# A perceiver layer with two routed expert stages: one block for both parts, and TensorE in slots of one gated unit with the down product of a unit inside the next

## The chip, the cores and the metric

The kernel runs on one core of one Trainium2 chip. The metric is device time in microseconds (us) of one execution. The core's engines run their own instruction streams in parallel and meet through semaphores: TensorE (PE; PEld is its weight load) for matrix products, VectorE (DVE), ScalarE (ACT), GpSimd (POOL) and SyncE (SP), which here only issues transfers.

## The reference, cut to what matters

`x` is 64 sequences of 32 tokens by 256 channels, so 2048 tokens. One layer is computed: cross attention, a time mix with a first mixture of experts (two choices per token of 8), and a second feed-forward stage with a shared gated unit and one routed gated unit per token:

```python
        def geglu(x, w1, w2, w3):
            return jax.nn.gelu(x @ w1, approximate=False) * (x @ w2) @ w3
        B, T, C = x.shape
        xf = x.reshape(-1, C)
        shared = geglu(xf, w1s, w2s, w3s)
        logits = xf @ Wg
        idx = jnp.argmax(logits, axis=-1)
        final = jnp.zeros_like(xf)
        for e in range(N_EXPERTS):
            y = geglu(xf, W1[e], W2[e], W3[e])
            final = final + jnp.where((idx == e)[:, None], y, 0.0)
        return (shared + final).reshape(B, T, C)
    x = x + _L0_xattn_ref(_layernorm(x, axis=-1), ctx_1024, ...)
    x = x + _L0_attn_ref(_layernorm(x, axis=-1), ...)
    x = x + _L0_ffn_ref(_layernorm(x, axis=-1), ...)
```

w1 and w2 are 256 x 1024, w3 is 1024 x 256, all float32. `_L0_attn_ref` ends in the first mixture of experts. The kernel computes only the chosen expert of each token.

## The kernel before

The 2048 tokens are G = 16 chunks of 128. **Part 1** (cross attention, time mix, first experts in NT1 = 39 tiles of 128 rows) is one block of code; its last steps store expert rows to `rows_y` in DRAM (L476). The block ends with a barrier, the semaphores are cleared (L1486, L1487), and **part 2** follows as three blocks.

The *combine block* (L1722 on) takes a chunk a step. GpSimd copies the chunk's row numbers (L1754) and gathers the two expert rows of each token (`ya`, `yb2`, L1757). VectorE adds them weighted, takes mean and variance; GpSimd takes the inverse root (L1762); VectorE writes the normed `z4` (L1828); SyncE stores it to `rows_z` (L1742). TensorE transposes `z4` into bank `bZ` (L1777), ScalarE copies that to `zT_c` (L1800), and TensorE forms the router's 8 scores (L1785). In the same step TensorE runs the shared unit: `Geglu.hidden` (L1691: 32 products, 64 instructions with the two passes of float32, in two halves of u and g), ScalarE's GELU (L1700), VectorE's product (L1708), and `Geglu.down` (L1715: 8 products). The order on TensorE in a step is hidden products of unit n, transposes of the next chunk, down product of unit n - 1, router. Only SHARED_C = 12 of the 16 chunks have their shared unit here, one step behind; the last four chunks pass through without one.

The *table block* (`routing`) begins when all scores are there. VectorE takes the largest score of each token, counts tokens per expert by two products on TensorE, makes the slot of each token (each expert's rows padded to whole tiles of 128), and builds with one-hot products a table `table2` of which token sits in which row of the NT2 = 23 tiles. One shared unit runs beside it.

The *routed block* takes a tile a step. GpSimd copies a table column (L1920) and gathers 128 rows of `rows_z` (`zr`, L1922). TensorE's order in a step is the 32 hidden products of tile n (weights `we12`), the transposes of tile n + 1 (L1941), the down product of tile n - 1 (weights `we3`); ScalarE copies the transposes (L1979). SyncE loads the expert's weights, 3 MB a tile, two tiles deep (L1893, L1902): the 2 MB of `we12` wait for the hidden products of two tiles before, the 1 MB of `we3` for the down product of two tiles before. Results go to `rows_f` (L1984). One shared unit runs at the front and two at the end. Then GpSimd gathers each token's row of `rows_f` for 16 chunks (L1931), VectorE adds them (L2018), SyncE stores the output (L1913).

In part 1 the lists of tokens are made in another way, which the change takes over: each chunk's token numbers are scattered to a table in DRAM, `tab_e`, by GpSimd (L724); VectorE makes from the counts which expert and which place in the table each tile has (L1348 to L1371); SyncE reads each tile's 128 entries back with an address from a register (`moe_pick`, L344).

`Step` and `sweep` write loops: some steps peeled, the rest in a hardware loop.

## Time and profile before

| | us |
|---|---|
| median of 3 runs | 974.52 (973.53 to 974.78) |
| profiled execution, its own time | 966.43 |
| its span, first to last instruction | 964.7 |
| mean granted clock of TensorE | 0.953 |
| TensorE busy | 858.3 (89%) |
| VectorE busy | 445.0 (46%) |
| ScalarE busy | 316.3 (33%) |
| GpSimd busy | 349.3 (36%) |

Busy time is a union over the instructions of an engine; TensorE's instructions overlap in its pipeline. The granted clock is a share of full speed: 1.00 is the higher of two levels. The profile was taken on an execution of its own, so its span is compared with its own time and not with the median. Part 1 takes the first 485 us, the combine block stands from about 489 to 644, the table block to 668, the routed block to 944, and the last gathers and stores to the end.

### The profile page before, as it was taken

How to read it: one execution, taken by the hardware profiler on the slowest of the kernel's cores; microseconds unless marked ns; L12 is line 12 of the kernel's file. 1: busy time of each engine (PE TensorE's matmuls, PEld its weight loads, DVE VectorE, ACT ScalarE, POOL GpSimd, SP SyncE). 2: the span in 40 equal slices, each digit the busy share in tenths (PEclk: the TensorE clock that was granted, in tenths of full speed). 3: DMA queues.
4: the chain of work that ended last, by engine and by line, in shares of the span. 5: the costliest groups of instructions: out<-in, count | busy, mean ns of one | idle time of the engine just before them, and what ended most of it. 6: DMA issues, size and time to landing. Idle time of an engine off the chain costs nothing. (4 is left out here: it accounts for less than half of the span.)

```text
span 964.7 us, 19179 instructions
## 1 busy us (share of the span) xinstructions
PE 858.3 (89%) x6306; PEld 768.6 (80%) x6306; DVE 445.0 (46%) x1253; ACT 316.3 (33%) x712; POOL 349.3 (36%) x605
## 2 busy tenths in 40 slices
PE   5899989886667999999949999968999999999994
PEld 4567766665566889999849999957999999999993
DVE  1279989888774555555523333353111111111113
ACT  1466767664542445555411111100111111111110
POOL 1445677766775355544142222211100010000006
PEclk9899999998688989999979999989999999999998
DMA  9875557534612322263121111102998988999716
GB/s 355 277 268 189 194 112 233 155 103 188 169 43 53 79 67 83 83 214 84 50 66 33 34 38 40 38 28 73 336 330 305 329 301 324 303 319 306 270 61 175
DMA packets 92096, 161.79 MB, mean 168 GB/s; under 512 B 13832, under 2 KB 71112, under 8 KB 88680
## 3 DMA queue, kind: packets, MB, share of 16 engines
q1 hardware_dynamic: 71008, 103.39, 32.2%
q10 hardware_dynamic: 12832, 37.82, 10.5%
q0 software_dynamic: 8176, 19.57, 7.9%
q8 instruction: 43, 0.70, 0.3%
q14 instruction: 37, 0.30, 0.1%
HBM read 146.10 MB, written 14.66 MB: 167 GB/s over the span
## 5 line engine op out<-in xcount | busy, mean ns | idle before, releaser
L1691 PEld LDWEIGHTS bank<-zT_f,we 128*128 128x128 f32 x1472 | 167.9, 192 | 1.8 <-ACT zT_f L1979 0.7
L1691 PE MATMUL bank<-zT_f,we 128*128 128x128 f32 x1472 | 168.2, 275 | 0.5 <-ACT zT_f L1979 0.5
L1708 DVE TENSOR_TENSOR hT_f<-bank,act_g 128x512 f32<-128x512 f32 x78 | 53.8, 691 | 227.6 <-PE bank L1691 208.0
L1700 ACT ACTIVATE act_g<-bank 128x512 f32<-128x512 f32 x78 | 46.6, 597 | 320.4 <-PE bank L1691 320.4
L1691 PE MATMUL bank<-zT_c,a_x 128*128 128x128 f32 x1024 | 121.4, 281 | 0.3 <-PEq L1521 0.3
L1691 PEld LDWEIGHTS bank<-zT_c,a_x 128*128 128x128 f32 x1024 | 119.2, 197 | 0.8 <-issue 0.7
L361 POOL DMA_INDIRECT arena_a<-rows_e,pick x78 | 76.0, 975 | 29.8 <-issue 29.8
L410 PE MATMUL bank<-arena_b,arena_a 128*128 128x128 f32 x624 | 81.8, 288 | 1.6 <-DVE hT L546 1.6
L1715 PE MATMUL bank<-we,hT_f 128*128 128x256 f32 x368 | 83.2, 379 | 0.0
L410 PEld LDWEIGHTS bank<-arena_b,arena_a 128*128 128x128 f32 x624 | 78.2, 204 | 2.4 <-DVE arena_b L538 2.4
L1715 PEld LDWEIGHTS bank<-we,hT_f 128*128 128x128 f32 x368 | 68.1, 190 | 8.3
L437 PE MATMUL bank<-arena_a,hT 128*128 x312 | 73.8, 379 | 0.7 <-DVE arena_a L552 0.7
L1920 POOL COPY pick_f<-table 128x1 uint32 (+1 forms) x23 | 4.2, 184 | 186.3 <-PE bank L1941 159.1
L437 PEld LDWEIGHTS bank<-arena_a,hT 128*128 128x128 f32 x312 | 59.2, 190 | 9.2 <-issue 1.1
L1715 PE MATMUL bank<-t_w,hT_f 128*128 128x256 f32 x256 | 59.9, 388 | 3.7 <-DVE hT_f L1708 3.7
L827 PE MATMUL bank<-arena_b,t_w 128*128 128x128 f32 x384 | 55.3, 298 | 6.8 <-DVE arena_b L1230 3.5
L827 PEld LDWEIGHTS bank<-arena_b,t_w 128*128 128x128 f32 x384 | 49.7, 207 | 13.0 <-issue 13.0
L1715 PEld LDWEIGHTS bank<-t_w,hT_f 128*128 128x128 f32 x256 | 48.6, 195 | 10.5 <-DVE hT_f L1708 4.3
L538 DVE SCALAR_TENSOR_TENSOR arena_b<-arena_b,mu_e 128x128 f32<-128x128 f32 x156 | 44.4, 347 | 6.5 <-issue 6.3
L464 ACT ACTIVATE arena_a<-arena_a 128x1024 f32 x39 | 41.2, 1057 | 10.7 <-issue 10.6
L1762 POOL TENSOR_TENSOR rs<-var,eps_pow 128x1 f32<-128x1 f32 x16 | 9.1, 571 | 93.2 <-DVE var L1821 93.2
L1931 POOL DMA_INDIRECT x<-rows_f,slot x16 | 15.5, 970 | 73.5 <-DMA rows_f<-yr 68.9
(273 smaller groups left out, 1361.8 us busy)
## 6 DMA issues: line engine op xcount, KB each, us to landing
we<-in_W_dram SPq DMA_DIRECT2D x69, 1024.0 KB, 7.4
arena_a<-in_ctx_n_dram ACTq DMA_DIRECT2D x16, 1152.0 KB, 7.2
arena_a<-in_ctx_t_dram SPq DMA_DIRECT2D x16, 1028.0 KB, 9.0
rows_y<-arena_a ACTq DMA_DIRECT2D x39, 128.0 KB, 1.7
arena_a<-in_w_moe_dram ACTq DMA_DIRECT2D x3, 1156.0 KB, 5.3
arena_a<-in_w_moe_dram ACTq DMA_DIRECT2D x3, 1152.0 KB, 7.5
rows_f<-yr ACTq DMA_DIRECT2D x23, 128.0 KB, 6.3
rows_e<-arena_b SPq DMA_DIRECT2D x64, 32.0 KB, 4.0
```

The source lines that it names most:

```text
L361: nc.gpsimd.indirect_dma_start(out=pair[:, n % NM, i * D:(i + 1) * D], out_offset=None, in_=rows_e.ap()[0:rows + 1, :], in_offset=bass.Ind ...
L410: last = nc.tensor.matmul(bMH[:, f * P:(f + 1) * P], wk_e[:, n % 2, k * FK + f * P:k * FK + (f + 1) * P], xk[:, n % 2, k * P:(k + 1) * P], ...
L437: last = nc.tensor.matmul(bMY[:, 0:D], hT[:, n % 2, f * P:(f + 1) * P], ewv_sb[:, e, f * D:(f + 1) * D], start=f == 0, stop=f == FKC - 1)
L464: nc.scalar.activation(wk_e[:, n % 2], ewk_sb[:, e], ACT.Copy).then_inc(m_awk, 1)
L538: last = nc.vector.scalar_tensor_tensor(o[:, n % 2, h], diffT[:, n % 2, h], mu_e[:, n % NM, i, k:k + 1], prevT[:, n % 2, h], ALU.mult, ALU ...
L827: last = nc.tensor.matmul(bank[:, m * P:(m + 1) * P], t_w[:, i, k, m * P:(m + 1) * P], xm[:, n % 2, i, k], start=k == 0, stop=k == KD - 1)
L1691: last = nc.tensor.matmul(bank[half][:, f * P:(f + 1) * P], w12[:, i, k, col0:col0 + P], zT[:, k], start=k == 0, stop=k == KD - 1)
L1700: nc.scalar.activation(act_g[:, half], bU[half][:], ACT.Gelu).then_inc(self.ac_g, 1)
L1708: nc.vector.tensor_tensor(hT[:, parity, half * HH:(half + 1) * HH].rearrange("p f t -> p (f t)"), bG[half][:], act_g[:, half], ALU.mult).t ...
L1715: last = nc.tensor.matmul(bY[parity][:, 0:D], hT[:, parity, f], w3[:, f], start=f == 0, stop=f == HC - 1)
L1762: nc.gpsimd.tensor_tensor(rs4[:, b.slot], var4[:, b.slot], eps_pow[:], ALU.pow).then_inc(po_r, 1)
L1931: nc.gpsimd.indirect_dma_start(out=yg[:, c], out_offset=None, in_=rows_f[:, :], in_offset=bass.IndirectOffsetOnAxis(ap=slot2[:, 0, c:c + 1 ...
```

## The change

Part 2 moves into the block of part 1, without loops: no barrier or semaphore clearing lies between, and its tiles lie in the memory of part 1's. The combine block and the table block are replaced. The 16 chunks form 9 groups (chunk 0, chunk 1, then pairs). TensorE, ScalarE and VectorE go through 39 slots, each one gated unit: shared chunks 0 to 10, routed tile 0, shared chunk 11, routed tiles 1 to 22, shared chunks 12 to 15. In a slot TensorE runs the first half of the hidden products, the down product of the unit before, the second half, and then, in the first 8 slots, transposes and router products of the next group; before a routed tile, the transposes of that tile. The ranks of each group's tokens among those with the same expert are products on TensorE (`ranks`), and GpSimd scatters each chunk's token numbers to a table in DRAM, `tab_f`. SyncE reads the 23 lists back one by one (`pick_rows`) and then loads weights as before; GpSimd waits for all 23 before it gathers tile 0. The final gathers and additions stand among the last four slots. Semaphores of part 1 are merged in places, and the reads of its lists are waited for in other groups; nothing else of part 1 moves.

```diff
-                        before, after = s.back(1, NT2), s.back(-1, NT2)
-                        pe.wait_ge(ac_z, s.n + 1)
-                        w, lap = weights_of(s)
-                        pe.wait_ge(got_w12[w], lap * 32 + 32)
-                        ge.hidden(pe, unit_r(s)[0], zT[:, s.offset % 2], we12[:, w])
-                        if after:
-                            transpose_z(after)
-                        if before:
-                            down_routed(before)
...
-        nc.clear_and_free_semaphores(one_sems)
-        nc.all_engine_barrier()
...
+        GROUPS = [(0, 1), (1, 2)] + [(c, c + 2) for c in range(2, G, 2)]
+        NGR = len(GROUPS)
+        NT2 = (TOK - E) // P + E
+        SLOTS = ([("s", c) for c in range(NGR + 2)] + [("r", 0), ("s", NGR + 2)]
+                 + [("r", n) for n in range(1, NT2)] + [("s", c) for c in range(NGR + 3, G)])
...
+            def pick_rows(n):
+                at = sp.value_load(place2[0:1, n:n + 1], min_val=0, max_val=T_ROWS // P - 1)
+                sp.dma_start(pick2[:, n], tab_f[bass.ds(at * P, P), :]).then_inc(f_pick, 16)
+            sp.wait_ge(c_dv_map, 1)
+            load_w12(0)
+            sp.wait_ge(c_po_tab, 16 * G)
+            for n in range(NT2):
+                pick_rows(n)
+            for n in range(1, NT2):
+                load_w12(n)
+                load_w3(n - 1)
+            load_w3(NT2 - 1)
...
+            def gather_tile(n):
+                need(pool, c_pe_z, NGR + n - NZ + 1 if n >= NZ else 0)
+                nc.gpsimd.indirect_dma_start(out=zr[:, n % NZ], out_offset=None, in_=rows_z[:, :],
+                                             in_offset=bass.IndirectOffsetOnAxis(ap=pick2[:, n, 0:1], axis=0)
+                                             ).then_inc(got_tile[n][0], 16)
+            gather_sums(0)
+            gather_sums(1)
+            for i in range(-1, NGR):
+                if i + 1 < NGR:
+                    rstd(i + 1)
+                if i + 3 < NGR:
+                    gather_sums(i + 3)
+                if i >= 0:
+                    list_rows(i)
+            pool.wait_ge(c_put, G * 16)
+            pool.wait_ge(f_pick, 16 * NT2)
+            for n in range(NT2):
+                gather_tile(n)
+            pool.wait_ge(c_dv_row, 1)
+            for n in range(NT2 - NF, NT2):
+                pool.wait_ge(*put_tile[n])
...
+            def transposed(g):
+                lo, hi = GROUPS[g]
+                pe.wait_ge(c_dv_z, hi)
+                need(pe, c_ac_z, g)
+                for c in range(lo, hi):
+                    for k in range(KD):
+                        last = nc.tensor.transpose(bZ[:, ((c - lo) * KD + k) * P:((c - lo) * KD + k + 1) * P],
+                                                   z4[:, c, k * P:(k + 1) * P], ident[:])
+                last.then_inc(c_pe_z, 1)
+
+            def router(g):
+                lo, hi = GROUPS[g]
+                pe.wait_ge(c_ac_z, g + 1)
+                need(pe, c_dv_prod, g)
+                for c in range(lo, hi):
+                    for k in range(KD):
+                        last = nc.tensor.matmul(bL[:, (c - lo) * E:(c - lo + 1) * E], zT_c[:, c, k], r2_w[:, k],
+                                                start=k == 0, stop=k == KD - 1)
+                last.then_inc(c_pe_l, 1)
...
+            transposed(0)
+            pe.wait_ge(ld_s, 16 * 4)
+            router(0)
+            for i in range(NSLOT):
+                hidden(i, 0)
+                if i > 0:
+                    down(i - 1)
+                if i < NGR:
+                    ranks(i)
+                hidden(i, 1)
+                if i + 1 < NGR:
+                    transposed(i + 1)
+                if in_slot(i + 1, "r") is not None:
+                    transpose_z(in_slot(i + 1, "r"))
+                if i + 1 < NGR:
+                    router(i + 1)
+            down(NSLOT - 1)
...
+            copy_z(0)
+            router(0)
+            for i in range(NSLOT):
+                gelu(i, 0)
+                gelu(i, 1)
+                store(i - 1)
+                if i + 1 < NGR:
+                    copy_z(i + 1)
+                if in_slot(i + 1, "r") is not None:
+                    copy_tile(in_slot(i + 1, "r"))
+                if i + 1 < NGR:
+                    router(i + 1)
...
+            combine(0)
+            normed(0)
+            for i in range(NSLOT):
+                if i + 1 < NGR:
+                    combine(i + 1)
+                if i < NGR:
+                    largest(i)
+                products(i, 0)
+                if i >= 1:
+                    take(i - 1)
+                if i == NSLOT - 1:
+                    finish(1)
+                if i < NGR:
+                    places(i)
+                if i + 1 < NGR:
+                    normed(i + 1)
+                if i == NGR - 1:
+                    tile_map()
+                products(i, 1)
+                if i == NGR:
+                    row_numbers()
+                if i == NSLOT - 2:
+                    finish(0)
+            finish(2)
+            dve.drain()
+            take(NSLOT - 1)
...
```

**TensorE, routed tiles, before.** L1691 are hidden products, L1941 transposes of the next tile, L1715 the down product of the tile before.

```order
L1691 MATMUL bank<-zT_f,we 128x128 x32
L1941 MATMUL bank<-ident,zr 128x128 x2
L1715 MATMUL bank<-we,hT_f 128x256 x8
L1691 MATMUL bank<-zT_f,we 128x128 x32
L1941 MATMUL bank<-ident,zr 128x128 x2
```

Now, at the same place; L1627 are hidden products, L1640 the down product, L1610 the transposes (part 2's tiles carry the names of the memory they lie in: `arena_a`, `arena_b`).

```order
L1610 MATMUL bank<-ident,arena_b 128x128 x2
L1627 MATMUL bank<-arena_b,arena_a 128x128 x16
L1640 MATMUL bank<-arena_a,arena_b 128x256 x8
L1627 MATMUL bank<-arena_b,arena_a 128x128 x16
L1610 MATMUL bank<-ident,arena_b 128x128 x2
L1627 MATMUL bank<-arena_b,arena_a 128x128 x16
L1640 MATMUL bank<-arena_a,arena_b 128x256 x8
L1627 MATMUL bank<-arena_b,arena_a 128x128 x16
L1610 MATMUL bank<-ident,arena_b 128x128 x2
```

The down product moved from between the transposes and the next hidden products into the middle of the hidden products; transposes and the products on their copy are neighbours.

**TensorE, shared units with chunks to prepare, before.** One step of the combine block; L1777 are the transposes, L1785 the router products.

```order
L1691 MATMUL bank<-zT_c,a_x 128x128 x32
L1777 MATMUL bank<-ident,z 128x128 x2
L1715 MATMUL bank<-t_w,hT_f 128x256 x8
L1785 MATMUL bank<-r_w,zT_c 128x8 x2
L1691 MATMUL bank<-zT_c,a_x 128x128 x32
```

Now, for a pair of chunks; L1579 are the transposes, L1589 the router, L1598 to L1601 the rank products.

```order
L1627 MATMUL bank<-arena_b,a_x 128x128 x16
L1640 MATMUL bank<-t_w,arena_b 128x256 x8
L1598 MATMUL bank<-mask,before_m 128x8
L1601 MATMUL bank<-earlier,ones_m 128x8
L1598 MATMUL bank<-mask,before_m 128x8
L1600 MATMUL bank<-mask,ones_m 128x8
L1601 MATMUL bank<-earlier,ones_m 128x8
L1627 MATMUL bank<-arena_b,a_x 128x128 x16
L1579 MATMUL bank<-ident,arena_a 128x128 x4
L1589 MATMUL bank<-r_w,arena_b 128x8 x4
L1627 MATMUL bank<-arena_b,a_x 128x128 x16
```

Here too the down product no longer stands between transposes and router, and two chunks are prepared at once.

**SyncE, ahead of the first routed tiles, before:** the store of `z` and then weights.

```order
L1742 DMA rows_z<-z 128x256
L44 REGISTER_ALU
L44 COMPARE_AND_BRANCH
L1737 UNCONDITIONAL_BRANCH
L1884 UNCONDITIONAL_BRANCH
L1887 TENSOR_LOAD expert
L1887 ISA x2
L1893 ISA
L1893 DMA we<-in_W_dram 128x2x1024 x2
```

Now, with the first of 23 reads of a list (`pick` from `tab_f`):

```order
L1483 DMA rows_z<-arena_a 128x256 x16
L1486 TENSOR_LOAD expert
L1486 ISA x2
L1490 ISA
L1490 DMA arena_a<-in_W_dram 128x2x1024 x2
L1499 TENSOR_LOAD place
L1499 ISA x2
L1500 ISA
L1500 DMA pick<-tab_f 128x1
```

Each read takes a place from a table into a register and then issues a transfer; 23 of them stand between the first tile's weights and the second's.

## Rows read from the trace of the kernel before

**Rows 1.** Windows: start:end, us, busy of PE, PEld, DVE, ACT, POOL, PEclk, DMA share, GB/s

```profile
505.00:633.00 128.00, 127.19 (x976) 122.44 (x975) 44.95 (x117) 18.34 (x35) 30.38 (x46) 1.00 0.12 35
633.00:668.00 35.00, 22.10 (x137) 19.53 (x135) 19.66 (x99) 2.35 (x5) 3.19 (x4) 0.80 0.07 19
690.00:925.00 235.00, 235.00 (x1784) 226.05 (x1783) 39.33 (x65) 34.31 (x65) 19.82 (x35) 1.00 0.88 307
925.00:964.70 39.70, 26.17 (x182) 24.09 (x180) 10.90 (x24) 2.39 (x4) 15.53 (x16) 0.89 0.39 113
```

**Rows 2.** Timeline, part 1 to part 2: start, us, engine, line, op [idle before <-releaser]

```profile
480.29 5.22 ACTq L476 DMA_DIRECT2D rows_y<-arena_a  x3
...
489.48 0.99 POOL L1757 DMA_INDIRECT ya<-rows_y,pick_c  x1 [0.50 <-POOL pick_c L1754]
...
498.84 9.02 PE L1691 MATMUL bank<-zT_c,a_x 128*128 128x128 f32 x64
```

**Rows 3.** Timeline, hidden products of one shared unit

```profile
576.91 7.39 PE L1691 MATMUL bank<-zT_c,a_x 128*128 128x128 f32 x64
```

**Rows 4.** Timeline, a chunk prepared without a unit beside it

```profile
638.61 0.44 PE L1777 MATMUL bank<-ident,z 128*128 128x128 f32 x2 [0.49 <-DVE z L1828]
...
639.08 0.38 ACT L1800 ACTIVATE zT_c<-bank 128x256 f32<-128x256 f32 x1 [4.35 <-PE bank L1777]
...
639.52 0.61 PE L1785 MATMUL bank<-r_w,zT_c 128*128 128x8 f32 x4 [0.47 <-ACT zT_c L1800]
```

**Rows 5.** Timeline, front of the routed block and two later tiles

```profile
668.40 7.38 PE L1691 MATMUL bank<-zT_c,a_x 128*128 128x128 f32 x64 [0.32 <-PEq L1521]
...
687.34 0.38 PE L1941 MATMUL bank<-ident,zr 128*128 128x128 f32 x2
...
687.76 0.38 ACT L1979 ACTIVATE zT_f<-bank 128x256 f32<-128x256 f32 x1 [1.41 <-PE bank L1941]
...
688.20 7.41 PE L1691 MATMUL bank<-zT_f,we 128*128 128x128 f32 x64 [0.47 <-ACT zT_f L1979]
...
699.12 7.31 PE L1691 MATMUL bank<-zT_f,we 128*128 128x128 f32 x64
...
709.94 7.31 PE L1691 MATMUL bank<-zT_f,we 128*128 128x128 f32 x64
```

**Rows 6.** Lists in part 1: timeline, one tile view, page's issues (count, KB, landing)

```profile
302.76 0.98 POOL L724 DMA_INDIRECT tab_e<-token,listed  x1 [0.30 <-issue]
...
304.47 0.29 DVE L1348 TENSOR_TENSOR scratch<-bank,tile_lo 128x128 f32<-128x128 f32 x1 [4.43 <-PE bank L933]
...
307.86 0.25 DVE L1371 SCALAR_TENSOR_TENSOR place<-te_f,taken_a,tb_f 128x30 int32<-128x30 f32 x1
...
308.85 33.01 SPq L344 DMA_DIRECT2D pick<-tab_e  x30
...
L344 SPq DMA_DIRECT2D pick<-tab_e x39: 337/338/402, 239.0 to 341.5; - x39
...
we<-in_W_dram SPq DMA_DIRECT2D x69, 1024.0 KB, 7.4
...
pick<-tab_e SPq DMA_DIRECT2D x39, 1.0 KB, 1.8
...
zr<-rows_z,pick_f POOLq DMA_INDIRECT x23, 6.6
ya<-rows_y,pick_c POOLq DMA_INDIRECT x16, 2.8
```

**Rows 7.** Timeline, the last units and the end

```profile
926.09 7.31 PE L1691 MATMUL bank<-zT_c,a_x 128*128 128x128 f32 x64
...
936.69 7.31 PE L1691 MATMUL bank<-zT_c,a_x 128*128 128x128 f32 x64
...
950.48 3.72 PE L1715 MATMUL bank<-t_w,hT_f 128*128 128x256 f32 x16 [3.03 <-DVE hT_f L1708]
...
962.13 0.43 DVE L2018 TENSOR_TENSOR xz<-xz,x 128x256 f32<-128x256 f32 x1 [0.92 <-DMA x<-rows_f,slot]
```

870 lines of the change are left out of this document (335 added, 535 removed).

## The prediction

> **What bounds the kernel now.** I read the windows first. In the routed stage, 690:925 [rows 1], TensorE is busy 235.00 of 235.00 us at granted clock 1.00, while VectorE has 39.33 and the DMA engines are at 0.88: the stage is as long as its matmuls. The same holds for the combine stage (127.19 of 128.00). TensorE has slack in three places: before the first unit (from the last row store at 485.5 to the first products at 498.84 [rows 2]), in 633:668, where it works 22.10 of 35.00 us at clock 0.80 while VectorE makes the tables [rows 1], and after 925 (26.17 of 39.70). So the change can win only there, some 12 + 13 + 13 us at most, and whatever it adds between two matmuls elsewhere is paid in full. I then read the time order around one unit: with its transposes it takes 709.94 - 699.12 = 10.82 us [rows 5], without them 936.69 - 926.09 = 10.60 [rows 7], so two transposes whose copy is covered cost 0.22. A slot of the changed kernel without extras is the same 10.60: same 32 products and 8 down products.
>
> I build the new time line in the clock of the old trace (span 964.7).
>
> **Start.** Barrier and semaphore clearing go. The last store begins at about 485.2 (480.29 + 5.22 less its own 0.3) and lands, like other small transfers (1.8 for the reads of [rows 6]), near 486.9; the gather then starts after 0.5 (the idle before the one at 489.48): 487.4 instead of 489.48. The chain gather, combine, square root, transpose, copy, router has the same steps and took 498.84 - 489.48 = 9.36 [rows 2]. First products at 496.7. Bounds: 0 and 4 us gained; I take 2.1.
>
> **Slots 0 to 7, the added wait.** Before, the down product stands between the transposes and whatever needs their copy (order, first place). Now the router products follow the transposes at once. The trace has this case once per chunk where no unit is left: transposes at 638.61, copy on ScalarE at 639.08, router at 639.52, that is 0.91 us, then 0.61 of router [rows 4]. With two chunks: 0.22 more for two transposes, about 0.2 more for a copy of twice the columns, and eight router instructions instead of four, about 1.1: 0.91 + 0.22 + 0.2 + 1.1 = 2.45. The rank products (five small ones in bf16, 8 columns each) lie between nothing and the router's 0.61; I take 0.2, nearer to nothing, since they are half as wide in bytes and wait for nothing. Slot = 10.60 + 2.45 + 0.2 = 13.25. Slot 0 has no down product, but the first products ran 9.02 us after the idle stretch [rows 2] against 7.39 warm [rows 3]: 9.02 + 0.91 + 0.61 + 0.2 = 10.75. So slot 1 starts at 507.4, and slot 8 at 507.4 + 7 x 13.25 = 600.2. VectorE does about 3.75 us per chunk and unit (44.95 us over some 12) [rows 1]; doubled, with ranking, it stays under 10 in 13.25, and every step on it is wanted late in the slot: not the bound.
>
> **Slots 8 to 10.** 10.60 + 0.35 of ranks, then 10.60 twice: TensorE wants routed tile 0 at 632.4.
>
> **The wait that replaces the table block.** Tile 0 can't be gathered before all 23 lists of rows are read back, and these not before all 16 chunks are listed. Last ranks at 600.2 + 7.2 = 607.4; VectorE takes the unit and does three short steps, 608.7; two scatters on GpSimd, the second at 610.3. Its landing lies between a gather's 2.8 [rows 6] and 5.3 (308.1, where the map ended, less 302.76; SyncE's read followed 0.74 later): 613.1 to 615.6. The map takes 308.11 - 304.47 = 3.6, so 612.3, and SyncE issues two weight loads after it. One load of the place register later (0.74: 308.85 after 308.11) the first read is issued, at about 615.0. Thirty such reads took 33.01 us: (33.01 - 0.34)/29 = 1.13 each [rows 6]. Last of 23: 615.0 + 22 x 1.13 = 639.8; landed + 1.8 = 641.6; GpSimd waits for all of them, + 0.5 = 642.1; a tile gather lands 6.6 later while weights load, and SyncE starts 3 MB of weights at 640.5; 2.8 if they didn't matter [rows 6]. 648.7. So TensorE stands 16.3 us (12.5 to 18). Queued behind this on SyncE are load_w12(1) and load_w3(0); their unit and its down product come some 20 us later, so they are covered. After the stop the first products run at the low level again, as at 498.84 (granted clock 0.80 in 633:668 shows the same): + 1.8. Transposes and copy 0.86 + 0.2 at the low clock: slot 11 begins at 649.8 and takes 12.4: 662.2.
>
> The Trainium skill, DMA: Bandwidth & Descriptors, section on latency and other measured facts, gives HBM access as 0.2 us on average and 2 us at high load. By that the loaded gather would be 2.8 + 1.8 = 4.6 and the end 2.0 earlier; the row says 6.6, with 128 rows each, and I stay with it.
>
> **Routed slots, the added wait.** Moving the down product to the middle of the next unit takes away what hid the copy of the next tile. The trace shows the bare sequence once: transposes 687.34, copy 687.76, products 688.20 [rows 5]: 0.86 instead of 0.22, with TensorE idle 0.47 of it. Slot = 10.60 + 0.86 = 11.46, up to 11.57 if the restart costs 0.1; I take 11.5. It occurs before each of r1 to r22: slot 12 and slots 13 to 33. 662.2 + 22 x 11.5 = 915.2. Weights: 3.1 MB in 11.5 us where it was 10.8; the load of a unit now has one slot and the copy wait, about 12 us, to land, was 7.4 in the median [rows 6]: covered, with 4 us to spare.
>
> **End.** Slots 34 to 38 are 5 x 10.60: the last hidden products end at 968.2. The 16 final gathers and additions now run under four shared units instead of behind the last. What is left: product 1.0, down 3.72, addition 0.2 + 0.42, store 964.7 - 962.56 = 2.1 [rows 7]: 7.5 with rounding. Before, 944.0 to 964.7 was 20.7. End at 975.7, span + 11.0.
>
> **Sum against the old points.** Thirteen units are done at 668.40 before [rows 5] and at 662.2 + 11.5 = 673.7 now: + 5.3, of which the start gives - 2.1 and the slots with the stop + 7.4. From there to the last hidden product: 944.0 - 668.4 = 275.6 before, 21 x 11.5 + 5 x 10.60 = 294.5 now, + 18.9: copy waits 21 x 0.68 = 14.3, one down product that stood after 944.0 (3.5), the rest rounding. End 7.5 against 20.7: - 13.2. In all + 11.0. The profiled execution's own time was 966.43, the median 974.52. I add 11.0 to the median: **985.5 us**, 1.1% slower.
>
> **Rivals.**
> A, faster: **the lists are read in time.** If SyncE issues reads back to back at the 0.338 us of the instruction itself [rows 6], the last one goes at 622.4, tile 0 is there at 631.3, before 632.4. No stop and no slow products: 16.3 + 1.8 less, 967.4. It decides at (632.4 - 8.9 - 615.0)/22 = 0.39 us a read. Against it: both series in the trace ran at 1.13, since each read first loads a register from the table. The Trainium skill, DMA: Bandwidth & Descriptors, section on issuing engines, calls the sequencer's time to start a DMA "usually small relative to the DMA itself"; that is this rival, and the trace disagrees for reads of an address out of a register. Chance 0.09.
> B, faster: **the copy wait is hidden**, for instance because the first weight load runs ahead and the copy comes in under the pipeline's tail. 22 x 0.64 = 14 and some 5 in the group slots less: 967 to 971. Against: the products read the copied tile, and at 688.20 they waited. Chance 0.08.
> C, slower: **weights come late.** Both loads of a slot are now issued together at its end; at the stage's 307 GB/s with the tiles' traffic 3.5 MB take 11.4. If the last of them gates the next unit, slots are 12.1: + 13, 998. Chance 0.08.
> D, slower: **the group slots stretch** behind VectorE or GpSimd (six indirect transfers of 1.3 a slot, 8 of 13.25): + 1 a slot moves the list too, + 8: 993. Chance 0.10.
> E, **no change**: the stop and the copy waits are each about two thirds of what I count (33 us in all, 11 less) and the gains cancel them: 974.5 within 2 us. Chance 0.08.
> Forecast 0.57.
>
> **Numbers.** 0.2% (2 us) is about what a measurement can tell from no change. Faster: A, B and the low edge of E, 0.19. Same: most of E and a little of the forecast's own doubt, 0.06. Slower 0.75, from the forecast, C and D. The forecast's own bounds (gather 2.8 to 7.8, scatter, start, 0.1 per routed slot) give 979 to 991. The range goes down to 970, leaving out A, and up to 996, leaving out C.
>
> **What will show it.** First products of part 2 near 497. An idle stretch of TensorE of 12 to 18 us before the first routed tile, ended by a gather, with SyncE issuing 23 reads 1.13 apart ahead of it, and a low clock after it. Routed period 11.5 with ScalarE's copy ending an idle time of 0.5 in each. Under 8 us from the last hidden product to the end. I am wrong if the reads come faster than 0.6 us apart (then it is no slower), or if the routed period is 10.8.

## The result, and the profile after

The changed kernel took **1009.79 us** (1007.30 to 1013.65) beside 974.28 us (973.53 to 974.78) of the kernel before: ratio 1.0369, 95% interval 1.0333 to 1.0404, 35.5 us slower where 11 were predicted. Its profiled execution took 1008.72 us, with a span of 1007.0.

The windows of after, cut by its own stages (start:end, us, busy of PE, PEld, DVE, ACT, POOL, granted clock, DMA share, GB/s); they answer to [rows 1]:

```profile
505.00:600.00 95.00, 86.00 (x621) 80.32 (x619) 43.84 (x167) 12.61 (x26) 38.04 (x41) 0.93 0.27 51
600.00:650.00 50.00, 45.44 (x351) 43.17 (x351) 16.66 (x63) 5.74 (x11) 4.65 (x5) 0.98 0.24 49
650.00:680.00 30.00, 13.37 (x81) 12.59 (x81) 1.12 (x2) 1.58 (x3) 3.87 (x4) 0.63 0.38 124
680.00:940.00 260.00, 249.59 (x1850) 235.04 (x1849) 41.17 (x68) 35.32 (x67) 18.14 (x19) 1.00 0.82 279
940.00:1007.00 67.00, 56.02 (x376) 51.53 (x374) 14.32 (x31) 5.37 (x9) 15.29 (x16) 0.92 0.22 67
```

TensorE now idles in every stage: 9 us in the first window, 5 and 17 around the first routed tile, 10 in the routed stage, 11 after 940. What ended those waits, by the view of waits of PE from 485 on (for whom, total, times, longest):

```profile
PE bank L1610 <- DMA arena_b<-rows_z,pick: 20.0, 1, 20.0
PE bank L1579 <- DVE arena_a L1730: 11.0, 2, 10.4
PE bank L1627 <- ACT arena_b L1679: 10.9, 23, 0.5
PE bank L1627 <- issue: 9.4, 13, 1.8
PE bank L1589 <- ACT arena_b L1666: 7.2, 9, 1.4
```

The first is the stop ahead of routed tile 0; the third the copy of each tile, 23 times 0.47 us; the fifth the same at the routers. The second is the start. The fourth the prediction doesn't have: hidden products of a unit whose weights and rows lie in SBUF, and that wait for nothing the profile shows. Such a stretch is called one without a shown wait below.

The stop and the products behind it, in time order (start, us, engine, line, operation [idle before and what ended it]): the last scatter of the lists, tile 0's weights, the 23 reads, TensorE:

```profile
623.71 0.97 POOL L1541 DMA_INDIRECT tab_f<-token,listed  x1 [0.30 <-issue]
625.92 0.92 SPq L1490 DMA_DIRECT2D arena_a<-in_W_dram  x2
632.79 24.93 SPq L1500 DMA_DIRECT2D pick<-tab_f  x23
666.15 0.66 PE L1610 MATMUL bank<-ident,arena_b 128*128 128x128 f32 x2 [20.03 <-DMA arena_b<-rows_z,pick]
667.28 6.08 PE L1627 MATMUL bank<-arena_b,arena_a 128*128 128x128 f32 x32 [0.47 <-ACT arena_b L1679]
```

The next lines are one routed tile: transposes, copy on ScalarE, products, the half-way down product, the other half; before, such a tile had no idle time [rows 5]. The next copy's wait ends at 737.90, 11.55 later:

```profile
725.49 0.38 PE L1610 MATMUL bank<-ident,arena_b 128*128 128x128 f32 x2
725.91 0.38 ACT L1679 ACTIVATE arena_b<-bank 128x256 f32<-128x256 f32 x1 [1.41 <-PE bank L1610]
726.35 3.84 PE L1627 MATMUL bank<-arena_b,arena_a 128*128 128x128 f32 x32 [0.47 <-ACT arena_b L1679]
730.02 3.62 PE L1640 MATMUL bank<-arena_a,arena_b 128*128 128x256 f32 x16
733.48 3.73 PE L1627 MATMUL bank<-arena_b,arena_a 128*128 128x128 f32 x32
737.90 3.84 PE L1627 MATMUL bank<-arena_b,arena_a 128*128 128x128 f32 x32 [0.47 <-ACT arena_b L1679]
```

And the stretch without a shown wait, late in the kernel. GpSimd issues the sixteen gathers of the routed rows, one in 1.26 us, from 956.55 on; eleven microseconds later PE's products come one at a time:

```profile
957.81 0.95 POOL L1568 DMA_INDIRECT x<-rows_f,slot  x1 [0.30 <-issue]
962.70 4.86 PE L1627 MATMUL bank<-arena_b,a_x 128*128 128x128 f32 x41
968.02 0.27 PE L1627 MATMUL bank<-arena_b,a_x 128*128 128x128 f32 x1 [0.46 <-issue]
968.73 0.37 PE L1627 MATMUL bank<-arena_b,a_x 128*128 128x128 f32 x1 [0.44 <-issue]
975.10 0.59 PE L1627 MATMUL bank<-arena_b,a_x 128*128 128x128 f32 x2 [1.76 <-issue]
979.36 2.29 PE L1627 MATMUL bank<-arena_b,a_x 128*128 128x128 f32 x10 [0.42 <-issue]
```

64 products take from 962.70 to 981.44, 18.7 us; warm and undisturbed they take 7.14. The last gather is issued at 975.4, and at 979.4 PE runs freely again. Smaller stretches of the kind stand at 523 and at 565 to 569, behind rows of four gathers (515.64 to 519.47 and 558.73 to 562.60).

The end, to be held against [rows 7], is short as forecast: the last down product starts at 1000.67, its addition at 1004.43, end 1007.0.

### The profile page after: what moved, and what is told of

The parts are those of the page before. It is cut to its first block, busy times and chain, and to the rows that moved or that the text cites. A ratio compares the mean times of both kernels' runs of the same rounds, so it can differ in the third digit from the quotient of the medians.

```text
span 1007.0 us, 18812 instructions
## 1 busy us (share of the span) xinstructions
PE 875.5 (87%) x6328; PEld 777.8 (77%) x6328; DVE 443.8 (44%) x1278; ACT 316.3 (31%) x714; POOL 355.2 (35%) x572
## 3 DMA queue, kind: packets, MB, share of 16 engines
q1 hardware_dynamic: 74464, 103.47, 31.8%
## 4 chain that ended last, share of the span: by engine, by line
PE 60%; DVE 11%; issue 6%; POOL 5%; DVEq 5%; DMA 4%; another core or an unknown queue 3%; ACT 3%; SPq 2%; ACTq 1%; POOLq 0%
PE bank L1627 26%; PE bank L1640 12%; PE bank L368 6%; PE bank L395 6%; PE bank L382 3%; DMA xz<-in_x_dram 2%; DVE arena_b L1189 2%; DVEq L1386 1%; POOL tab_e L683 1%; PE bank L357 1%; PE bank L1589 1%; SPq L1499 1%; SPq L1500 1%; PE bank L777 1%
## 5 line engine op out<-in xcount | busy, mean ns | idle before, releaser
L1627 PE MATMUL bank<-arena_b,arena_a 128*128 128x128 f32 x1472 | 176.4, 279 | 10.9 <-ACT arena_b L1679 10.9
L1627 PEld LDWEIGHTS bank<-arena_b,arena_a 128*128 128x128 f32 x1472 | 171.9, 194 | 17.7 <-ACT arena_b L1679 16.5
L1807 DVE TENSOR_TENSOR arena_b<-bank,arena_b 128x512 f32<-128x512 f32 x78 | 53.9, 692 | 266.1 <-PE bank L1627 231.6
L1691 ACT ACTIVATE arena_b<-bank 128x512 f32<-128x512 f32 x78 | 46.6, 597 | 366.2 <-PE bank L1627 311.4
L1627 PE MATMUL bank<-arena_b,a_x 128*128 128x128 f32 x1024 | 131.6, 289 | 9.4 <-issue 9.4
L1627 PEld LDWEIGHTS bank<-arena_b,a_x 128*128 128x128 f32 x1024 | 126.7, 203 | 11.6 <-issue 11.2
L368 PE MATMUL bank<-arena_b,arena_a 128*128 128x128 f32 x624 | 82.4, 289 | 1.6 <-DVE hT L505 1.6
L1640 PE MATMUL bank<-arena_a,arena_b 128*128 128x256 f32 x368 | 83.2, 379 | 0.0
L368 PEld LDWEIGHTS bank<-arena_b,arena_a 128*128 128x128 f32 x624 | 78.8, 205 | 2.5 <-DVE arena_b L497 2.4
L1640 PEld LDWEIGHTS bank<-arena_a,arena_b 128*128 128x128 f32 x368 | 68.2, 190 | 8.3
L1640 PE MATMUL bank<-t_w,arena_b 128*128 128x256 f32 x256 | 58.6, 382 | 0.9 <-DVE arena_b L1807 0.9
L786 PEld LDWEIGHTS bank<-arena_b,t_w 128*128 128x128 f32 x384 | 48.5, 203 | 13.7 <-issue 13.6
L1640 PEld LDWEIGHTS bank<-t_w,arena_b 128*128 128x128 f32 x256 | 47.9, 192 | 7.0 <-DVE arena_b L1807 1.0
```

Source lines behind the costliest of these rows:

```text
L368: last = nc.tensor.matmul(bMH[:, f * P:(f + 1) * P], wk_e[:, n % 2, k * FK + f * P:k * FK + (f + 1) * P], xk[:, n % 2, k * P:(k + 1) * P], ...
L786: last = nc.tensor.matmul(bank[:, m * P:(m + 1) * P], t_w[:, i, k, m * P:(m + 1) * P], xm[:, n % 2, i, k], start=k == 0, stop=k == KD - 1)
L1627: last = nc.tensor.matmul(bank[half][:, f * P:(f + 1) * P], w12[:, i, k, col0:col0 + P], zT[:, k], start=k == 0, stop=k == KD - 1)
L1640: last = nc.tensor.matmul(bY[u % 2][:, 0:D], hT_f[:, u % 2, f], w3[:, f], start=f == 0, stop=f == HC - 1)
L1691: nc.scalar.activation(act_g[:, half], bU[half][:], ACT.Gelu).then_inc(g_ac_g, 1)
L1807: nc.vector.tensor_tensor(hT_f[:, u % 2, half * HH:(half + 1) * HH].rearrange("p f t -> p (f t)"), bG[half][:], act_g[:, half], ALU.mult). ...
```

## Experiments: the two costs that the prediction had

**One part undone: the down product back behind both hidden halves.**

```diff
                 hidden(i, 0)
-                if i > 0:
-                    down(i - 1)
...
                 if in_slot(i + 1, "r") is not None:
                     transpose_z(in_slot(i + 1, "r"))
+                if i > 0:
+                    down(i - 1)
                 if i + 1 < NGR:
                     router(i + 1)
```

(ScalarE's store and VectorE's taking of the result move with it.)

> The changed kernel with one part undone: the down product of the last unit stands behind both halves of the hidden products and the transposes, where it stood before, and the copy of the transposed rows goes ahead of the store on ACT. Theory (the copy wait is paid because nothing but the next unit's own products is left behind the transposes): the 0.47 us in which PE waits for the copy of each routed tile goes, and the period falls from 11.56 to about 10.8, 22 x 0.74 = 16 us; the nine waits of the routers for the copies in the shared slots (7.2 us) shrink too, to 2 or less: about 990 us from the changed kernel's 1009. Rival (the half-way placement also hides the products of DVE, so moving it back opens a wait of the same size at the down product): the period stays within 0.2 us of 11.56 and the time within 5 us. The stop ahead of the first routed tile (20 us) stays in either case, as do the stretches in which PE waits for nothing shown.

Measured: 994.44 us beside 970.93, ratio 1.0256 (1.0206 to 1.0307). The chain of work that ended last shows the routed tiles without a gap, 10.82 us each:

```profile
693.02 7.14 PE bank L1627 x64
700.17 0.22 PE bank L1610 x2
700.38 3.46 PE bank L1640 x16
703.84 7.14 PE bank L1627 x64
```

From 680 to 950 PE waits for nothing. So the copy wait is what the half-way down product costs: 23 x 0.74 = 17 us, less 3.5 because two down products now stand behind the last hidden ones. The time fell by less, about 1% (from 1.0369, or 1.034 to 1.035 in later runs, to 1.0256). One reason is that the stretches without a shown wait had 14.7 us of idle time in this run, against 9.8 in the changed kernel. Another is small: the routers' waits for the copies fell from 7.2 to 2.5 us, but 3.9 us of waits for VectorE ahead of the rank products came in their place. So the half-way down product hid something too, in the shared slots alone.

**The lists of the first two tiles read ahead of the others.**

```diff
+            for n in range(EARLY_N):
+                pick_rows(n)
+            load_w12(1)
+            load_w3(0)
-            for n in range(NT2):
+            for n in range(EARLY_N, NT2):
                 pick_rows(n)
...
-            pool.wait_ge(f_pick, 16 * NT2)
+            pool.wait_ge(f_pick0, 16 * EARLY_N)
             for n in range(NT2):
+                if n == EARLY_N:
+                    pool.wait_ge(f_pick, 16 * (NT2 - EARLY_N))
```

(EARLY_N is 2.)

> The changed kernel with the reads of the lists split: the lists of the first two routed tiles are read first and have their own semaphore, then the second tile's weights are loaded, then the other 21 lists are read. Theory (PE's 20.0 us stop ahead of the first routed tile is the row of 23 reads at 1.12 us and the gather behind them): the first gather starts 21 x 1.12 = 23.5 us earlier, at 637, its rows are there by 643, before PE is at 646, and the whole stop goes: 18 to 22 us less, 988 to 991. Rival (the reads' landing is late too, so the stop is only shortened): 8 to 14 us less. Second rival (the rows of the third tile, whose gather now waits for the other 21 lists, come too late): the stop moves to the third routed tile; its rows would be asked for near 665, and PE is there near 677, so nothing or up to 3 us.

Measured: 979.78 us, 1.0105 (1.0069 to 1.0141) beside the same runs of before. The changed kernel's ratios in other sets of runs (1.0343 to 1.0369) are 23 to 26 us above that, where 18 to 22 were expected. The first gather starts at 631.58, and the tile's transposes follow PE's work with no idle time, its products at full speed:

```profile
631.58 0.99 POOL L1552 DMA_INDIRECT arena_b<-rows_z,pick  x1 [14.44 <-DMA pick<-tab_f]
638.43 0.38 PE L1617 MATMUL bank<-ident,arena_b 128*128 128x128 f32 x2
639.29 3.84 PE L1634 MATMUL bank<-arena_b,arena_a 128*128 128x128 f32 x32 [0.47 <-ACT arena_b L1686]
```

The stop was the row of reads. Its price is the 20.0 us of waiting and 2.2 of slow products behind it (6.08 against 3.84); the rest, 1 to 4 us, I put down to the stretches in the shared units, which come and go; that isn't shown. Beside 3 MB of weights a read took (27.71 - 0.34)/20 = 1.37 us, not 1.12, and nobody waited for it.

## Experiments: the cost that it lacked

Theory 1 was **code**: part 2 is now written out in a line, the 16 KB blocks of PE's instructions arrive on a queue of their own, and gathers hold them up. First, the last gathers held back:

```diff
+            pool.wait_ge(g_pe_g, 2 * NSLOT)
             for (lo, hi), (landed, _) in zip(Y_PARTS, got_y):
```

> The changed kernel with the sixteen gathers of the routed rows on the software queue held back until the last hidden products are done. Theory (the stretch from 962.7 to 981.4, in which 64 products of one unit took 18.7 us instead of 7.1, comes from the sixteen gathers that run back to back there, which hold up the code that PE must still fetch): that slot takes 7.1 again, the last hidden products end near 988 instead of 999.7, and the end is then set by the gathers, 988 + 16 x 1.26 + 4, about 1012, so much the same time as now. Rival (code in a straight line stalls by itself, whatever the queues do): the slow stretch stays where it is, near 963, and the time rises to 1024. Second rival (PE's records show a stretch of a disturbed clock): the place moves or vanishes with the run, and the last hidden products end anywhere between.

Measured: 1017.51 us, 1.0496 (1.0458 to 1.0534). The slot that took 22 us takes 10.6, so the stretch belongs to the gathers. But this run can't tell what PE does during them: VectorE's additions stand in front of its last product and wait for the gathers, so PE had nothing left to do (23.2 us of idle time ended by L1808).

Then sixteen gathers more, among the routed tiles:

```diff
             for n in range(NT2):
+                if n == 12:
+                    for c in range(G):
+                        nc.gpsimd.indirect_dma_start(out=yg[:, c], out_offset=None, in_=rows_y[:, :],
+                                                     in_offset=bass.IndirectOffsetOnAxis(ap=slot1[:, 0, c:c + 1], axis=0)
+                                                     ).then_inc(f_extra, 16)
                 gather_tile(n)
...
```

> The changed kernel with work added: sixteen gathers of 128 rows back to back on the software queue ahead of the gather of the thirteenth routed tile, in the middle of the routed tiles, into a place that nothing reads before it is written again. PE has the rows of the next tiles already and waits for none of it. Theory (a burst of such gathers holds up the fetching of PE's straight-line code): PE stands still in steps of under 2 us with nothing shown that it waits for, 8 to 14 us in all, during or just behind the 20 us of the burst, and the time rises by that. Rival (the stalls have nothing to do with the gathers): the period of the tiles in the burst stays within 0.5 us of 11.56. Second rival (the burst costs by slowing the weights' loads, which take 77% of the queues' time here): PE waits for the weights of one or two tiles, shown as such.

Measured: 1016.27 us, 1.0467 (1.0431 to 1.0503). The copies behind the down products start at 759.65, 773.62, 797.47 and 809.02: periods of 13.97 and 23.85 instead of 11.56, 14.7 lost, and no weight load is waited for. Gathers are the cause wherever they stand.

PE isn't the only engine that is held up. Most of the loss here is a wait of PE for ScalarE's copy, 12.39 us instead of 0.47, and ScalarE's own step just ahead of that copy came 13.4 us late: it starts at 761.43 in the tile before and at 786.36 here, where one period of 11.56 later would be 772.99. VectorE starts the product after it at 787.97 [13.92 idle].

```profile
761.43 0.60 ACT L1697 ACTIVATE arena_b<-bank 128x512 f32<-128x512 f32 x1 [6.43 <-PE bank L1633]
786.36 0.60 ACT L1697 ACTIVATE arena_b<-bank 128x512 f32<-128x512 f32 x1 [19.80 <-remote]
788.38 5.59 PE L1633 MATMUL bank<-arena_b,arena_a 128*128 128x128 f32 x32 [12.39 <-ACT arena_b L1685]
```

("remote" is a releaser that the profile doesn't know.) Whether it goes by code was the next question.

**The kernel before, with the same burst twice**, once while PE meets its code for the first time and once in its hardware loop (the gathers are those of the last diff).

```diff
-                    sweep(pool, NT2, FPEEL, NZ, body, FTAIL)
+                    for n in range(NT2):
+                        if n in (8, 16):
+                            for c in range(G):
...
+                            pool.wait_ge(f_extra, 16 * G * (n // 8))
+                        body(Step(0, n, NZ))
```

> The kernel before with work added: GpSimd's own instructions of the routed stage are written out in a line, and sixteen gathers of 128 rows run back to back on the software queue twice: ahead of the gather of routed tile 8, when PE is near tile 4 and still runs through code for the first time (16 KB of it are fetched every 16 us there, until 766), and ahead of that of tile 16, when PE is near tile 12 in its hardware loop, for which nothing is fetched between 768 and 910. Theory (the burst holds up the fetching of PE's code): the first burst costs PE 8 to 15 us in steps with no wait shown, the second nothing, all periods of tiles 10 to 16 staying at 10.82 within 0.3. Rival (a burst slows matmuls, semaphores or the memory whatever PE runs): both cost about the same. Second rival (neither costs anything: the stall in the changed kernel has another cause that the burst added there hit by chance): the time stays within 3 us of before's.

Measured: 969.07 us beside 966.34, 1.0029 (1.0006 to 1.0052); every tile took 10.82 us. In the same set of runs, on the same chip, **both parts undone at once** (the first two diffs together):

> The changed kernel with two parts undone at once: the down product behind both hidden halves and the transposes (the period then measured 10.82 instead of 11.56, 12.4 us less in all), and the lists of the first two tiles read ahead (the 20 us stop gone, 27 us less in all). Theory (the two costs are at different places and add up): 1007 - 12 - 27 = 968, or up to 4 less if the first part's gain was masked by chance stalls among the shared units; within 0.5% of the kernel before. Rival (the copy wait in the routed tiles was hiding something, weights that come late when the period falls to 10.82 together with an earlier start): over 975, with waits for weights shown at PE.

944.95 us, 0.9788 (0.9756 to 0.9819), 23 us under the 968 expected, with four undisturbed slots of 10.60 beside the last gathers and shared slots of 12.9. The spaced kernel (below) took 943.70 there, 0.9776 (0.9744 to 0.9808), and one with each four gathers cut in two, two ahead of the scatters and two behind them, 945.84, 0.9778 (0.9738 to 0.9819): no difference in time.

> As the spaced kernel, and the four gathers of each pair of chunks among the shared units are split, two ahead of the lists' scatters and two behind them. Theory (bursts of four cost PE the stretches with no wait shown among the shared units, 2 to 8 us in the kernels run so far): 2 to 6 us less than the spaced kernel, about 954. Rival (bursts of four are too short, and those stretches are chance or come with the number of gathers): within 2 us of the spaced kernel.

This chip is not wholly free of it, though. The trace of the last kernel has two shared slots of 14.1 and 18.3 us instead of 12.9, behind six transfers of GpSimd in a row, one in 1.3 us (537.17 to 543.63). VectorE stands for 3 us with nothing shown that it waits for, and PE waits for it:

```profile
553.89 0.18 DVE L1756 TENSOR_TENSOR hot<-iota_e,at 128x16 f32<-128x16 f32 x1 [3.03 <-issue]
555.44 0.18 PE L1612 MATMUL bank<-mask,before_m 128*128 128x8 bf16 x1 [4.31 <-DVE earlier L1764]
```

The code theory didn't explain why bursts cost nothing there, first time or not. The earlier runs had been on another chip. So four kernels ran again, unedited, side by side on a third:

> The changed kernel unedited, beside three others on one chip. So far the stretches without a shown wait stood in runs of one chip (the changed kernel with a burst added, 14.5 us, and in the last gathers 10 to 11 us) and not in runs of another (the kernel before with two bursts, 0; the kernel with both parts undone, 0 in its last gathers). Theory A (it is the chip or the core: some run PE's code through a burst of gathers, some don't): on this one chip all four kernels show the stop some 10 us behind the start of a burst, or none does. Theory B (it is the kernel, and so its code or what runs beside the burst): the changed kernel again loses 10 to 12 us of hidden products in the last gathers, with the ratio to before at 1.037 within 0.005.

> The changed kernel with sixteen gathers added among the routed tiles, unedited from its earlier run, where the burst cost 14.5 us. Theory A (the chip): as the other three on this chip, with a stop or without. Theory B (the kernel): 12 to 15 us lost in that one tile again.

> The kernel with both parts undone, unedited, 0.979 of the kernel before when it ran. Theory A (the chip): if the changed kernel stops in its last gathers here, this one does too and stands at 0.990 of before; if the changed kernel does not, this one is at 0.979 and the changed kernel at about 1.025. Theory B (the kernel): 0.979 again, with four slots of 10.60 us at the end, whatever the changed kernel does beside it.

> The kernel before with two bursts added, unedited, whose bursts cost PE nothing when it ran. Theory A (the chip): if the changed kernel and its burst stop here, the first burst costs PE 8 to 15 us here; the second, in the hardware loop, nothing if it is the code's way to the engine that is held up, the same if it is not. Theory B (the kernel): all periods stay at 10.82 us.

Here the changed kernel took 1007.34 us beside 973.63 (1.0343, 1.0325 to 1.0361), its copy with the burst 1021.06 (1.0490), the kernel with both parts undone 975.49 instead of 944.95 (1.0023, 1.0009 to 1.0038, where 0.990 was expected), and the kernel before with two bursts 1005.39, 31.8 us more than without. **It is not the kernel**: two unedited kernels lose nothing in their rows of gathers in one set of runs, and lose time in them in another. Each set was on one chip and each chip had one set, so a chip can't be told from a core of it or from the time of the run; below I call it the chip. The starts of the copy that follows each tile's down product give the periods. On the chip with stretches, around the first and the second burst (gathers' packets from 717 to 735 and 819 to 837):

```profile
716.13 0.42 DVE L2014 COPY yr<-bank 128x256 f32<-128x256 f32 x1 [2.91 <-PE bank L1715]
741.93 0.42 DVE L2014 COPY yr<-bank 128x256 f32<-128x256 f32 x1 [3.17 <-PE bank L1715]
817.66 0.42 DVE L2014 COPY yr<-bank 128x256 f32<-128x256 f32 x1 [2.91 <-PE bank L1715]
844.71 0.42 DVE L2014 COPY yr<-bank 128x256 f32<-128x256 f32 x1 [4.45 <-PE bank L1715]
```

25.80 and 27.05 us instead of 10.82, so 15.0 and 16.2 lost. The same kernel on the chip without:

```profile
709.38 0.42 DVE L2014 COPY yr<-bank 128x256 f32<-128x256 f32 x1 [2.91 <-PE bank L1715]
720.20 0.42 DVE L2014 COPY yr<-bank 128x256 f32<-128x256 f32 x1 [2.91 <-PE bank L1715]
```

And it isn't the fetching of code. The second burst falls into PE's hardware loop, and the queues between 800 and 850 carried no instruction packet at all:

```profile
q1 hardware_dynamic: 5832, 10.64, 59.4%
q0 software_dynamic: 918, 2.49, 15.2%
q10 hardware_dynamic: 569, 0.52, 3.0%
```

yet PE loses as much there as in code it meets for the first time:

```profile
825.44 0.37 PE L1691 MATMUL bank<-zT_f,we 128*128 128x128 f32 x1 [0.36 <-issue]
826.14 1.28 PE L1691 MATMUL bank<-zT_f,we 128*128 128x128 f32 x2 [0.33 <-issue]
```

(The Trainium skill, Runtime: NRT & Kernel Launch, section on instruction fetch mechanics, says that code is streamed in 16 KiB blocks and that this is mostly hidden. The traces agree: the changed kernel has 53 such packets on PE's queue instead of 43, and no stop of part 2 was found to be theirs.)

**How many, how fast, and of what kind.** Both on a fourth chip, which has the stretches; both kernels have the two parts undone.

```diff
+                if n in dose:
...
+                    for c in range(dose[n]):
+                        gather_extra(c)
...
+                if 9 <= n < 13:
...
+                    u = UNIT_R[n - 3]
+                    for j, s in enumerate((g_pe_u, g_pe_g, g_pe_u, g_pe_g)):
+                        pool.wait_ge(s, 2 * u + j // 2 + 1)
+                        gather_extra(4 * (n - 9) + j)
```

> The kernel with both parts undone, with 46 gathers added among the routed tiles, which nothing reads: 16 back to back ahead of tile 6, 16 spaced over four slots ahead of tiles 9 to 12 (each waits for the next half of PE's products, one in 2.7 us), 8 back to back ahead of tile 15, 4 ahead of tile 18 and 2 ahead of tile 21. The place of a stop is read from the periods of the tiles, 10.82 undisturbed. Theory (on some chips a row of gathers issued faster than about one in 1.3 us holds PE's instructions up after some 10 us of it, and lets go 1 to 2 us behind its end): 12 to 15 us for the first 16, under 1 us for the spaced 16, 0 to 3 us for the 8, 0 for the 4 and the 2. Rival (it is the sum of gathers that costs, about 0.8 us each, however they are spaced): 12 to 15 for each of the 16, 6 for the 8, 3 for the 4, 1.5 for the 2. If the chip is one of those that show no stop, all periods are 10.82, and the last gathers cost nothing either.

```diff
+                if n == 6:
+                    for c in range(G):
+                        nc.gpsimd.tensor_copy(yg[:, c], z4[:, c])
...
+                if n == 11:
+                    for c in range(G):
+                        nc.gpsimd.dma_start(yg[:, c], rows_y[c * P:(c + 1) * P, :]).then_inc(f_extra, 16)
+                if n == 16:
...
+                    for c in range(G):
+                        gather_extra(c)
```

> The kernel with both parts undone, with three rows of work added on GpSimd among the routed tiles, read by nothing: 16 copies of 128x256 without any transfer ahead of tile 6; 16 plain transfers of 128 KB from consecutive rows ahead of tile 11; 16 gathers by index back to back ahead of tile 16, as the control. Theory (what holds PE up is the gathers' row by row work on the software queue): 0 for the copies, 0 to 3 for the plain transfers, 12 to 15 us for the gathers. Rival 1 (GpSimd's activity as such takes something that PE needs): the copies cost too. Rival 2 (any transfers issued by GpSimd in a row do it): the plain transfers cost 8 or more.

What each row of added work cost, by the starts of the copies behind the down products (undisturbed period 10.82); a tile's own gather goes ahead of each row:

| added on GpSimd | lost, us |
|---|---|
| 16 gathers, one in 1.26 us | 13.7 (periods 24.02 and 11.37) |
| 16 gathers, one in 2.7 us on average, four in about 5 us and then a pause | 0.0 |
| 8 gathers, one in 1.26 us | 4.2 (0 to 3 expected) |
| 4 gathers; 2 gathers | 0.0; 0.0 |
| 16 copies of 128x256, no transfer | 0.0 |
| 16 plain transfers of 128 KB, one in 0.54 us | 0.6 |
| 16 gathers, one in 1.26 us (control) | 12.1 |

The 8 gathers and the control:

```profile
804.25 0.42 DVE L1842 COPY arena_b<-bank 128x256 f32<-128x256 f32 x1 [2.91 <-PE bank L1666]
819.30 0.42 DVE L1842 COPY arena_b<-bank 128x256 f32<-128x256 f32 x1 [4.02 <-PE bank L1666]
```

```profile
798.44 0.42 DVE L1839 COPY arena_b<-bank 128x256 f32<-128x256 f32 x1 [2.91 <-PE bank L1663]
821.41 0.42 DVE L1839 COPY arena_b<-bank 128x256 f32<-128x256 f32 x1 [0.71 <-PE bank L1663]
```

It isn't the sum that decides: sixteen spaced ones are free, eight in a row are not. (Rate and length of a row aren't told apart.) For the kind of work the test is weaker. The 16 copies took only some 6 us, and the row of plain transfers 8.65, less than the 9.8 of the eight gathers; so both rivals are made unlikely and not refuted.

**Spacing in the kernel itself.** The last gathers, all but the first two and the last two, wait for the next half of the hidden products; where all are spaced, each of the four of a pair of chunks does too:

```diff
+            steps = [(s, 2 * u + half + 1) for u in range(NSLOT - 3, NSLOT)
+                     for half in (0, 1) for s in (g_pe_u, g_pe_g)]
             for (lo, hi), (landed, _) in zip(Y_PARTS, got_y):
                 for c in range(lo, hi):
+                    if 2 <= c < 2 + len(steps):
+                        pool.wait_ge(*steps[c - 2])
```

> The kernel with both parts undone, and the sixteen last gathers spaced: from the third to the fourteenth each waits for the next half of the hidden products of the last three slots, about one in 2.6 us instead of one in 1.26. Theory (gathers issued back to back hold up PE's code): the slot that took 21.5 instead of 10.6 takes 10.6 to 14, 7 to 11 us less than without the spacing, about 958, unless the last gathers now end behind the last down product, which costs up to 3. Rival (any gathers there hold PE up in the same sum, spaced or not): the loss is spread over three slots and the sum stays at 11 us: 968. Second rival (the tail is bound by the gathers themselves, as in the kernel before, where the last hidden products end 20.7 us before the end): spacing makes it longer, 970 to 975.

> The kernel with both parts undone and the last gathers spaced, once more; its first run was on a chip on which gathers hold nothing up. Theory (spacing avoids the stop): the last slots take 10.6 to 12 us each here instead of 12.1 and 21.4 in a row, 8 to 11 us less than the kernel without the spacing on such a chip, at 0.990 to 0.994 of the kernel before. Rival (the sum of gathers costs, not their spacing): the loss is spread over three slots, the ratio 1.000 to 1.004 as without the spacing.

> As the kernel with the last gathers spaced, and the four gathers of each pair of chunks among the shared units spaced as well, each behind the next half of the products. Theory: on a chip where gathers hold PE up, the shared slots, which took 13.1 to 26.4 us each where 13.0 is undisturbed (28 us in all), take 13 to 14, and the kernel stands at 0.970 to 0.980 of the kernel before there; on one of the other chips at 0.977 as the kernel without. Rival (the sum counts): within 0.5% of the kernel with only the last ones spaced.

On the fourth chip, with both parts undone: last ones spaced 965.14 beside 972.21, 0.9938 (0.9916 to 0.9960), against 1.0023 without spacing on the third chip; all spaced **953.19**, 0.9792 (0.9751 to 0.9834). The last four slots take 10.6 us on average again. One shared slot still took 18.5 instead of 13 (540.54 to 559.03): GpSimd issued a row of six transfers, gathers and scatters, and one of four there, one in 1.3 us (531.80 to 538.27 and 545.10 to 548.98). A single row of four gathers had been free among the routed tiles; these were not.

The last pair takes away the bursts alone, on a fifth chip. The changed kernel stays as it is but for the waits ahead of its gathers; of the last sixteen, eight wait, and the last six still go in a row.

> The changed kernel with one thing edited: its gathers are spaced by waits for PE's progress, those of each pair of chunks among the shared units and the first ten of the last sixteen; the down product, the lists and everything else stay as in the changed kernel. Theory (gathers issued in a row hold PE up on most chips, and that is the part of the loss that the prediction lacked): the slot of 22 to 23 us in the last gathers takes 10.6, and the shared slots lose 3 to 10 us instead of 17 to 20, so the time falls from about 1.034 to 1.037 of the kernel before to 1.008 to 1.016; what stays is the stop of 20 us ahead of the first routed tile and the period of 11.56, which the prediction had. Rival (the stops move to the next gathers whatever their spacing): 1.030 or more.

> The changed kernel unedited, as the control on the same chip. Theory: 1.034 to 1.037 of the kernel before, with one slot of 22 to 23 us in the last gathers and 17 to 20 us lost in the shared slots; if this chip is one of those on which gathers hold nothing up, both kernels are within 3 us of each other, at about 1.012.

990.72 us, 1.0180 (1.0156 to 1.0204), against 1007.89, 1.0351 (1.0310 to 1.0391), in the changed kernel: **17.2 us** are the bursts' (1.008 to 1.016 was expected for the spaced one). From the copy of the last routed tile to the end the spaced kernel takes 44.0 us (from 943.53) and the control 54.8 (from 950.59); 7 us more lie ahead of that, among the first shared slots. Last windows of the one and of the other:

```profile
940.00:988.00 48.00, 42.74 (x305) 40.07 (x303) 13.11 (x29) 4.18 (x7) 15.58 (x16) 0.99 0.30 91
```

```profile
940.00:1006.00 66.00, 53.79 (x368) 50.23 (x366) 14.30 (x31) 5.37 (x9) 15.24 (x16) 0.92 0.22 68
```

Two shared slots of the spaced kernel still took 14.5 and 14.1 us on PE instead of 13.1: 2.4 us that spacing by halves didn't take away. By VectorE's copies they look longer, 16.3 and 15.9, each with a short one of 11.3 behind it. There VectorE was held up and PE hardly at all: the down product ends at 545.4, and its result, which is taken 3.65 us behind the product's start in an undisturbed slot, is taken 6.9 behind it:

```profile
541.82 3.62 PE L1651 MATMUL bank<-t_w,arena_b 128*128 128x256 f32 x16
548.70 0.42 DVE L1829 TENSOR_TENSOR xz<-bank,xz 128x256 f32<-128x256 f32 x1 [5.93 <-remote]
```

## Why the prediction was right and wrong

**Right, by its own steps.** The direction. The routed slot: 11.56 measured, 11.5 forecast, and it is the copy wait, since undoing it gives 10.82. The group slot: 13.09 undisturbed, 13.25 forecast. The reads: (24.93 - 0.34)/22 = 1.12 us each, 1.13 forecast; rival A's back to back reads don't happen, B's hidden copy neither, weights (C) came in time, and the stop and the copy waits were there in full (E). The end: 7.3 us behind the last hidden products, 7.5 forecast. In an undisturbed group slot neither VectorE nor GpSimd was the bound (D).

**The step that failed** is the one in "Slots 0 to 7" that made every slot as long as its own instructions and waits: 10.60 plus 2.45 plus 0.2, seven times, and 5 x 10.60 at the end. The sum had no term for other traffic. The changed kernel issues its gathers four in a row, with two scatters behind them, where before there were two gathers at a time, and lays sixteen gathers beside four shared units that before ran behind the last of them. On most chips such a row holds PE, ScalarE and VectorE up. I wrote that the last gathers "now run under four shared units instead of behind the last" and booked it as a gain of 13.2; the slot they run under grew from 10.60 to 22.0, with 0.8 more in the one ahead of it, and gave 12.2 of it back. Measured on their own, on another chip, the bursts are 17.2 us, beside the 24.3 between 985.5 and 1009.8, and 2.4 more stay in the spaced kernel's shared slots.

In the old trace's clock the span was forecast at 975.7 and came out at 1007.0, 31.3 more. By the starts on PE, the first products were 2.8 late; slot 0 took 1.4 more than forecast, slots 1 to 7 together 9.5 more, the stop with the slot behind it 4.3, the 22 routed periods 1.1, and the last five slots 12.3; the other two terms come to -0.1. So 21.8 of the 31.3 stand where the gathers go in rows. Between the medians it is only 24.3, because the yardstick (below) hid the rest.

**Terms mis-sized.** The stop was 20.03 us, not 16.3. The second scatter starts at 623.71, the first read at 632.79: 9.1 us where I had 4.7. SyncE's wait for the scatters ends only then, so they needed up to 8 us to land, with 2 MB of tile 0's weights issued at 625.92 in between; I took 2.8 to 5.3 from rows in which no weights moved. The products behind the stop lost 2.2, not 1.8. Slot 0 took 12.07 instead of 10.75: its hidden products ran 9.86 us, not 9.02, and its router waited 1.36 for the copy, not 0.47. The first products came at 499.51 instead of 496.7, mostly because part 1 ended 2.3 us later in this execution (487.0 against 484.7; between 483.8 and 491.9 in the others, unedited code), which is no part of the change.

**A wrong yardstick.** The kernel before was profiled at 966.43 us, 8 under its median of 974.52. I added my sum to the median without asking why. Of the chips used here one runs it at 966.3 and the others at 970.9 to 973.7; the one is the chip without stretches. Most likely the profiled execution was from such a chip, and a trace like that can't show what gathers cost. The end of part 1 points the same way: its last products start at 482.70 there, at 481.85 to 484.63 in the four traces of the chip without stretches, and at 484.02 to 489.87 in the fifteen others. That is argued from the times, not shown.

## What to carry to other kernels

Work moved under a busy engine isn't free because its queue is: count how fast a rearranged kernel issues indirect gathers, and space them (one in 2.7 us on average was free here, one in 1.26 was not after about eight). Copies on the way to the next unit's first product want a product behind them that doesn't need them; the down product was that, and moving it half a unit ahead cost 0.74 us a tile. Where a consumer needs the first of a row of small reads, give the first ones a semaphore of their own: that alone was worth more than the whole change was meant to move, and with the two other repairs the kernel is 2.1% faster than before.

## What the runs showed of the hardware

- Sixteen indirect gathers of 128 rows of 1 KB, one in 1.26 us, slow PE to about one weight load and product in 0.7 us or worse, from 8 to 11 us behind the start of the row to 1 to 4 us behind its end; 11 to 16 us are lost. It doesn't matter whether PE runs a loop or new code, or whether weights are loaded at the time.
- ScalarE and VectorE are held up in the same stretches: ScalarE by 13.4 us in the burst among the routed tiles, VectorE by 3.2 us (548.70 instead of 545.5) in a shared slot in which PE lost 1.4.
- It happens on four chips (or five, with the one of the first comparison). On one more, bursts of sixteen cost nothing, and one kernel's trace has 6.5 us of it in two shared slots. What GpSimd's gathers share with the instructions or semaphores of the other engines, and why one chip is nearly spared, stays open. The Trainium skill, DMA: Bandwidth & Descriptors, section on latency and other measured facts, says that the rings of software descriptors lie in SBUF behind ports that two of the DMA engines also use, and has crowding at those ports as its best guess for why these two are slow; it names no effect on PE, and no run here tests it.
- A read whose address comes out of a register takes SyncE 1.12 us each in a row, and 1.37 beside loads of weights; a small scatter issued just ahead of 2 MB of weights needed up to 8 us to land.
